# Pair pass of a four-layer graph network: row and square sums move from VectorE to TensorE, products keep six PSUM banks

## What is computed

```
hihj  = concatenate([x[src], x[dst]])                       # one row for each edge
exp_e = exp(silu(bn(hihj @ Wf + bf)))                       # one score for each edge
z     = silu(bn(einsum('ed,hdk->ehk', hihj, Wg) + bg))      # 128 values for each edge
h     = segment_sum(attention * z, dst);  out = bn(h) + x
bn(v) = (v - mean(v, axis=0)) * rsqrt(var(v, axis=0) + 1e-5) * gamma + beta
```

## Time and profile before

| | us |
|---|---|
| median of 3 runs | 12785.85 (12779.04 to 12810.68) |
| the profiled execution, its own time | 12782.4 |
| its span | 12780.6 |
| pair pass, from the first product (L1587) to the last reduction | 9613 to 11996 |

### The profile page before, as it was taken

The page is one execution under the profiler, slowest core; times in us unless marked ns, Lnnn a source line. Parts: engine busy times, 40 slices in busy tenths (PEclk is TensorE's granted clock), DMA queues, the critical chain, the costliest instruction groups (busy, mean ns, idle before and its releaser), DMA issues. The chain is left out here.

```text
span 12780.6 us, 88605 instructions
## 1 busy us (share of the span) xinstructions
PE 4468.3 (35%) x19462; PEld 2929.4 (23%) x19462; DVE 3466.1 (27%) x8115; ACT 3243.9 (25%) x7261; POOL 8419.5 (66%) x8885
## 2 busy tenths in 40 slices
PE   1222222432222223333333433333353333333587
PEld 0000000210000102111111322223352333333466
DVE  4000000200000111000000311212144565666799
ACT  3233333333333333233233300000020000101365
POOL 5666666566666665666666566666656666666698
PEclk5555555655555555555555555555575555555799
DMA  3222222222222223222222111111114444444444
GB/s 99 71 70 69 70 71 69 70 79 69 70 71 69 70 70 88 70 69 70 70 68 70 52 46 47 47 47 46 47 43 131 134 137 133 139 135 140 135 162 136
DMA packets 676226, 1070.09 MB, mean 84 GB/s; under 512 B 150832, under 2 KB 518725, under 8 KB 648853
## 3 DMA queue, kind: packets, MB, share of 16 engines
q0 software_dynamic: 329072, 676.05, 20.5%
q10 hardware_dynamic: 247712, 225.10, 5.4%
q1 hardware_dynamic: 98981, 163.50, 3.9%
HBM read 904.63 MB, written 161.05 MB: 83 GB/s over the span
## 5 line engine op out<-in xcount | busy, mean ns | idle before, releaser
L441 POOL DMA_INDIRECT big<-table_parts,tile_cols x4689 | 4452.7, 950 | 2339.9 <-issue 1390.5
L583 PE MATMUL psum<-big 128*128 x4992 | 1720.4, 470 | 4278.4 <-ACT big L541 2184.7
L441 POOL DMA_INDIRECT big<-ptable,tile_cols x1563 | 1521.4, 973 | 842.4 <-issue 464.5
L441 POOL DMA_INDIRECT big<-table,tile_cols x1563 | 1489.1, 953 | 729.4 <-issue 458.6
L583 PEld LDWEIGHTS psum<-big 128*128 128x128 bf16 x4992 | 596.5, 119 | 5125.3 <-issue 4914.7
L541 ACT ACTIVATE big<-big,ones 128x2048 bf16<-128x2048 bf16 x312 | 625.1, 2004 | 4401.6 <-remote 2958.0
L534 ACT ACTIVATE big<-iota_col,dl_tab 128x128 bf16<-128x128 f32 x4992 | 1513.0, 389 | 134.0 <-issue 99.4
L1587 PE MATMUL psum<-acc,big 128*128 x3328 | 891.0, 436 | 1488.6 <-issue 897.0
L651 PE MATMUL psum<-big 128*128 x3328 | 770.8, 361 | 1450.4 <-issue 1348.7
L563 DVE TENSOR_REDUCE acc<-psum 128x128 f32<-128x384 f32 (+1 forms) x196 | 109.5, 559 | 4173.3 <-remote 2631.0
L1587 PEld LDWEIGHTS psum<-acc,big 128*128 128x128 f32 x3328 | 729.2, 309 | 1650.1 <-issue 1639.6
(11 more groups left out here) (298 smaller groups left out, 4174.4 us busy)
## 6 DMA issues: line engine op xcount, KB each, us to landing
big<-dl_rows ACTq DMA_DIRECT2D x104, 1024.0 KB
zrows<-big ACTq DMA_DIRECT2D x104, 1024.0 KB
big<-zrows SPq DMA_DIRECT2D x104, 1024.0 KB
big<-table_parts,tile_cols POOLq DMA_INDIRECT x4689
table_parts<-big SPq DMA_DIRECT2D x42, 672.0 KB, 3.5
big<-table,tile_cols POOLq DMA_INDIRECT x1563
big<-ptable,tile_cols POOLq DMA_INDIRECT x1563
ptable<-big SPq DMA_DIRECT2D x14, 455.0 KB, 4.2
```

The costliest lines, as they stand in the source:

```text
L441: pool.indirect_dma_start(out=slots[:, t % (groups * GT), 0:width], out_offset=None, in_=tab, in_offset=bass.IndirectOffsetOnAxis(ap=idx_t ...
L583: last = nc.tensor.matmul(held, m, rows_t, start=False, stop=False, skip_group_check=True)
```

## The change

PE takes the sums. Two of the 8 PSUM banks become accumulators (`z_sum`, `z_sq_sum`, one partition, 4 x 128 columns each), and the products of the items go round the other six. In half q, after item 6, PE adds up half q - 1 by four products of a column of ones with a quarter of the half (4 items x 128 = 512 columns); after items 7, 9, 11 and 13 it adds up one quarter of the squares each. ACT squares quarter by quarter into two small buffers of their own, so it no longer waits for the store, and `zbuf` is not overwritten. DVE no longer reduces, and `half_sum` and `total` are gone. `load_dst` is issued for half q + 3 after the stores of half q, with its two waits moved inside. The statistics block folds the two accumulators by two reductions on one partition.

```
--- before.py
+++ after.py
@@ -23,7 +23,7 @@
 CW = 7
 ACW = F + 2
 ZW = ACW + 1
-Z_BANKS = 8
+Z_BANKS = 6
 PSLOTS = 4
 PASSES = 5
 LN_EPS = 1e-5
@@ -1494,20 +1494,25 @@
 
 
 
-        s_dl, s_compared, s_masked, s_in, s_part, s_summed, s_squared = (sem(n) for n in (
-            "z_dst", "z_dst_compared", "z_masks", "z_in_window", "z_half_summed", "z_totals", "z_squared"))
+        s_dl, s_compared, s_masked, s_in, s_summed, s_squared, s_sq_summed = (sem(n) for n in (
+            "z_dst", "z_dst_compared", "z_masks", "z_in_window", "z_summed", "z_squared", "z_squares_summed"))
         s_zout = [sem(f"z_out{h}") for h in range(2)]
         s_scores = sem("z_scores")
         no = 4
         items0 = no * NI
         onehot_t = onehot.rearrange("p (h u) f -> p h (u f)", h=2)
         dl_wide = work_flat.rearrange("p (h e) -> p h e", h=2)
-        totals = wide[:, 0:2, 0:F]
-        part = wide[:, 2:4, 0:F]
+        QUART = HALF // 4
+        QUARTS = HALF // QUART
+        squares = [big[:, RB + OB + WB + k * QUART * F:RB + OB + WB + (k + 1) * QUART * F].rearrange("p (u f) -> p u f", f=F) for k in range(2)]
+        assert 2 * QUART * F <= 224 + 11 * (NW + 1)
+        z_sum, z_sq_sum = (bank[Z_BANKS + k][0:1, 0:QUART * F].rearrange("p (u f) -> p u f", f=F) for k in range(2))
         in_win = sc16[:, 0:2, :]
         low = sc16[:, 2, :]
         PER = HALF // READY_STEP
-        SUM_AFTER, SQUARES_AFTER = 2, HALF - 2
+        SUM_AFTER = Z_BANKS
+        SQUARES_AFTER = [Z_BANKS + 1 + 2 * j for j in range(QUARTS)]
+        assert SQUARES_AFTER[-1] < HALF
         PARTS = HALF * P // 512
         ITEMS_PER_PART = HALF // PARTS
         with nc.Block() as block:
@@ -1532,21 +1537,6 @@
                         dve.wait_ge(s_in, q + 1)
                         nc.vector.scalar_tensor_tensor(in_win[:, q % 2, :], d, float(P), low, ALU.is_lt, ALU.mult).then_inc(s_masked, 1)
 
-                def half_sum(q, k):
-                    rows_of = zbuf[:, q % 2, :, 0:F].rearrange("p u f -> p f u")
-                    if k == 0:
-                        dve.wait_ge(s_added, PSLOTS + (q + 1) * HALF)
-                    else:
-                        dve.wait_ge(s_squared, q + 1)
-                    if q > 0:
-                        dve.wait_ge(s_summed, 2 * q - 1 + k)
-                    nc.vector.tensor_reduce(part[:, k, :], rows_of, AX.X, ALU.add).then_inc(s_part, 1)
-
-                def total(q, k):
-                    dve.wait_ge(s_part, 2 * q + k + 1)
-                    nc.vector.tensor_tensor(totals[:, k, :], totals[:, k, :], part[:, k, :], ALU.add).then_inc(s_summed, 1)
-
-                nc.vector.memset(totals, 0.0)
                 for j in range(PARTS):
                     compare(0, j)
                 for q in range(HALVES):
@@ -1557,6 +1547,8 @@
                     if q >= 2:
                         dve.wait_ge(s_zout[h], 16 * (q // 2))
                         dve.wait_ge(s_scores, q - 1)
+                        dve.wait_ge(s_summed, q - 1)
+                        dve.wait_ge(s_squared, (q - 1) * QUARTS)
                     for u in range(HALF):
                         n = q * HALF + u
                         if u % READY_STEP == 0:
@@ -1566,16 +1558,21 @@
                                                        bank[n % Z_BANKS][:, 0:ACW], ALU.mult, ALU.add).then_inc(s_added, 1)
                         if u % ITEMS_PER_PART == 1 and q + 1 < HALVES:
                             compare(q + 1, u // ITEMS_PER_PART)
-                        if q > 0 and u in (SUM_AFTER, SQUARES_AFTER):
-                            half_sum(q - 1, u // SQUARES_AFTER)
-                        if q > 0 and u in (SUM_AFTER + 1, SQUARES_AFTER + 1):
-                            total(q - 1, u // SQUARES_AFTER)
-                for k in range(2):
-                    half_sum(HALVES - 1, k)
-                    total(HALVES - 1, k)
 
             @block.tensor
             def _(pe):
+                def add_half(q):
+                    pe.wait_ge(s_added, PSLOTS + (q + 1) * HALF)
+                    for j in range(QUARTS):
+                        last = nc.tensor.matmul(z_sum, ones[:, 0:1], zbuf[:, q % 2, j * QUART:(j + 1) * QUART, 0:F],
+                                                start=q == 0 and j == 0, stop=False, skip_group_check=True)
+                    last.then_inc(s_summed, 1)
+
+                def add_squares(q, j):
+                    pe.wait_ge(s_squared, q * QUARTS + j + 1)
+                    nc.tensor.matmul(z_sq_sum, ones[:, 0:1], squares[j % 2], start=q == 0 and j == 0, stop=False,
+                                     skip_group_check=True).then_inc(s_sq_summed, 1)
+
                 for q in range(HALVES):
                     at = pair_values(pe, WIN, q, (NW - 1) * ACW)
                     for u in range(HALF):
@@ -1586,30 +1583,40 @@
                             pe.wait_ge(s_added, PSLOTS + n - Z_BANKS + 1)
                         nc.tensor.matmul(bank[n % Z_BANKS][:, 0:ACW], onehot_t[:, q % 2, u * P:(u + 1) * P],
                                          dyn(acc_flat, at[u], ACW), start=True, stop=True).then_inc(s_prod, 1)
+                        if q > 0 and u == SUM_AFTER:
+                            add_half(q - 1)
+                        if q > 0 and u in SQUARES_AFTER:
+                            add_squares(q - 1, SQUARES_AFTER.index(u))
+                add_half(HALVES - 1)
+                for j in range(QUARTS):
+                    add_squares(HALVES - 1, j)
 
             @block.scalar
             def _(act):
                 def load_dst(q):
+                    if q >= 2:
+                        act.wait_ge(s_compared, PARTS * (q - 1))
+                        act.wait_ge(s_dl, 16 * q)
                     act.dma_start(dl_wide[:, q % 2, :], dl_rows[q * HALF:(q + 1) * HALF, :].rearrange("i e -> (i e)").partition_broadcast(P)
                                   ).then_inc(s_dl, 16)
 
                 load_dst(0)
                 act.wait_ge(s_dl, 16)
                 load_dst(1)
+                load_dst(2)
                 for q in range(HALVES):
                     h = q % 2
-                    if q + 2 < HALVES:
-                        act.wait_ge(s_compared, PARTS * (q + 1))
-                        act.wait_ge(s_dl, 16 * (q + 2))
-                        load_dst(q + 2)
                     act.wait_ge(s_added, PSLOTS + (q + 1) * HALF)
                     act.dma_start(zrows[q], zbuf[:, h, :, 0:F]).then_inc(s_zout[h], 16)
                     nc.scalar.copy(score_tab[:, q * HALF:(q + 1) * HALF], zbuf[:, h, :, F])
                     nc.scalar.copy(weight_tab[:, q * HALF:(q + 1) * HALF], zbuf[:, h, :, SCW]).then_inc(s_scores, 1)
-                    act.wait_ge(s_zout[h], 16 * (q // 2 + 1))
-                    act.wait_ge(s_summed, 2 * q + 1)
-                    z = zbuf[:, h, :, 0:F]
-                    nc.scalar.activation(z, z, ACT.Square).then_inc(s_squared, 1)
+                    if q + 3 < HALVES:
+                        load_dst(q + 3)
+                    for j in range(QUARTS):
+                        n = q * QUARTS + j
+                        if n >= 2:
+                            act.wait_ge(s_sq_summed, n - 1)
+                        nc.scalar.activation(squares[j % 2], zbuf[:, h, j * QUART:(j + 1) * QUART, 0:F], ACT.Square).then_inc(s_squared, 1)
                 for h in range(2):
                     act.wait_ge(s_zout[h], 16 * (HALVES // 2))
                 act.wait_ge(s_dl, 16 * HALVES)
@@ -1619,19 +1626,22 @@
 
         s_v, s_root, s_wide, s_silu, s_exp, s_sums = (sem(n) for n in ("bn_steps", "bn_root", "bn_wide", "bn_silu", "bn_exp", "bn_sums"))
         mean, var, scale_r, shift_r = (rows[:, k, :] for k in (RT0, RT1, RT2, RT3))
-        z_stats = bank[5]
+        score_sums = bank[5][0:1, 0:2]
         scores_sq = work_flat[:, 0:NI]
         s_col, sq_col = (work_flat[:, NI + k:NI + k + 1] for k in range(2))
         with nc.Block() as block:
             @block.vector
             def _(dve):
-                step = Steps(dve, s_v, 0, 17)
+                step = Steps(dve, s_v, 0, 19)
                 step(nc.vector.tensor_reduce(s_col, score_tab, AX.X, ALU.add))
                 step(nc.vector.tensor_tensor(scores_sq, score_tab, score_tab, ALU.mult))
                 step(nc.vector.tensor_reduce(sq_col, scores_sq, AX.X, ALU.add))
                 dve.wait_ge(s_sums, 1)
-                step(nc.vector.tensor_scalar(mean, z_stats[0:1, 0:SCW], 1.0 / E, None, ALU.mult))
-                step(nc.vector.tensor_scalar(var, z_stats[0:1, SCW:2 * SCW], 1.0 / E, None, ALU.mult))
+                for row, sums, k in ((mean, z_sum, 0), (var, z_sq_sum, 1)):
+                    nc.vector.tensor_reduce(row[:, 0:F], sums.rearrange("p u f -> p f u"), AX.X, ALU.add)
+                    step(nc.vector.tensor_copy(row[:, F:SCW], score_sums[:, k:k + 1]))
+                for row in (mean, var):
```

(13 more changed lines are left out.)

## The result

The changed kernel takes 12845.0 us (12827.8 to 12853.6), the kernel before 12785.85 us: a ratio of 1.0044, 95% interval 1.0033 to 1.0055. It is slower by 59 us; 12696 us were forecast. The profiled execution took 12844.6 us (span 12842.8). Both kernels were run where queues creep, that is, where rows start far apart with nothing that holds them ("remote"), as the prediction describes. In some later sets of runs they don't, and the kernel before takes 11361 to 11377 us with nothing changed.

The account below looks back on a forecast made before the run. POOL was taken to set the pair pass's pace: 1985 us of gathers plus 359.5 us of waiting for slots. That wait's -91 and the statistics block's +1 gave -90, hence 12696 us (forecast's own range 12590 to 12760).

Parts of the forecast that it names:

- The sum: Pair pass: POOL's wait falls from 359.5 to 268.4 us, -91; with +1 for the statistics block, -90.
- Step 2: PE in the pair pass gains eight fp32 products a half; some 13 us a half, between 10.8 and 21.5.
- Step 3: Six banks for item products: DVE waits 1 to 4.5 us behind `add_half`; gain 0 to 7 us a half.
- Step 1: DVE in the pair pass loses reductions and adds, 832 us; 7.2 us a half remain, off a release's path.
- the ring: Pair pass slots, 32 against 64 in the weights pass: may keep more of POOL's wait, down to a gain of 30.
- rival B: PE becomes the bound at items 7 to 13 of each half: slower, 12870 us (12820 to 13100); chance 0.22.
- 1700 to 2200 named as a sign: PE's busy time in the pair pass, in us, expected after the change.
- Step 4: ACT squares in quarters, 4 x about 0.59 us for one of 1.92, without waiting for the store: costs nothing.
- Step 5: Last sums, after the last half's last add: 7 to 14 us, taken as 11, for 11.4 now; no change.
- Step 6: Statistics block: two reductions and two copies come in, two 128-column products go; +1 us (0 to 3).
- The gathers: Pair pass gathers are 0.02 us dearer than in the weights pass, 31 us in all, expected to stay.
- A: POOL's wait in the pair pass stays as it is: 12770 us, between 12750 and 12800; chance 0.20.

Follow-up runs that it names:

- fixed stretches: Constant reductions of fixed length put into DVE's queue, no creeping: kernel before 11952.4, changed 11693.4, one at a time 11561.9, without products 11372.3 us.
- holds: Stretches put into DVE's queue, of fixed length or until POOL stops: kernel before 11952.4 us (fixed, no creeping), 12939.8 us (until POOL stops, with creeping).
- the first edits: Changed kernel without products 11340.5, short products 11347.3, one at a time 11344.8; kernel before with six banks 11360.7; against 11361.8 us.
- the eight banks: Sums on TensorE with eight item banks kept, a 256-column product of ones ahead of each item product: 12862.8 us against 12791.9 of the kernel before.

## Why the prediction was wrong

The step that failed is its sum, "POOL's wait goes from 359.5 us to the 268.4 us of the pass whose consumer is light: -91". It went to 440.1. The sum has a term for DVE's lighter load and none for six banks and for the products of ones in PE's queue; steps 2 and 3 leave both to the sum, and the sum puts them at nothing. The runs with creeping give all three, as POOL's wait: six banks 359.5 to 433.6, +74; DVE's reductions gone 433.6 to 345.4, -88; the products of ones 345.4 to 440.1, +95; together +81. So the -91 was nearly right in size for what it stood for, and what failed is that the other two terms, +169 us, were left out.

- Step 1, DVE's load: 681 us busy in the pass, near the 600 named. "So DVE's work leaves the path of a release" is not what the runs show with creeping, where taking the reductions off won 133 us; without creeping DVE had not been on that path before either, since POOL never stopped.
- The level that the sum took from the weights pass, 268.4 us, was not reached even without any product: 345.4 us, with DVE at 673 us of work and six banks. That -88 is close to -91 is partly luck, since it is a fall from another level. The weights pass differs in 8 groups of slots for 4 and in a lighter DVE (428 us); I named the ring as a bound of the gain and did not follow it. Which of these holds the wait at 345 us was not tried.
- Step 2, PE's load: 9.3 us a half for the products (966/104) and 6.6 for the items, 15.9 in all, against the 13 of the estimate and its bounds of 10.8 and 21.5. The granted clock is 0.78 in the pass, and 0.86 without creeping: over the 0.75 under which rival B decides. PE's 1553 us in the pass lie under the 1700 to 2200 named as a sign.
 The Trainium skill's rule (TensorE: Matmul & The Clock Gate, section "HAM oscillation — how this bites in real kernels") holds in part here: one block of sums ran at 0.57, some 8 us after PE had stood 2.28 us for squares, and the one before it at 1.00.
- Step 3, six banks: PE's 3.5 to 7.0 us in `add_half` and DVE's wait of 1 to 4.5 us behind it were right in size (3.60 and 6.24; 2.96 and 5.15). "A gain of 0 to 7 us for a half" holds on the average of the pass: 8.0 us of reductions went, and DVE's waits for PE grew from 1.1 to 6.4 us a half (112.5 and 666.5 over 104), which leaves 2.7 us. But the fewer banks were priced only by that wait. In the kernel before they cost 77 us, though its waits for PE did not grow (86 us for 112).
- Step 4: ACT "costs nothing", but 303.6 us of PE's waits are for its squares; what they cost on the path was not tried. Step 5: from the last add to the last product 7 us, within 7 to 14, for 11.4. Step 6: from the first statistics reduction to the next stage's first operations 21.5 us before and 22.1 after, +0.6 for +1.
- The gathers: "31 us in all, I leave". Stops apart, the pass became 20 us shorter (2344.4 - 347.9 = 1996.5; 2389.0 - 413.0 = 1976.0), as the price of a gather fell from 973 to 959 ns. This was a gain left out.

In time, the same chain reads: two banks fewer +77; reductions away, with ACT's squares in quarters and `load_dst` moved along, -133; products one at a time +72; and +44 for the block of four and for the waits on the half's end and on ACT that the version one at a time also avoids. The last step compares two sets of runs. Each has some 20 us of uncertainty, and whether two banks cost the same where there are no reductions was not tried.

Of the rivals, B comes nearest in time and place: 12845 lies in its 12820 to 13100, and DVE's adds do wait for several hundred us (666.5) behind PE's queue. Its reason fails: the clock stood at 0.78, PE was busy for 1553 of 2391 us, and some of the loss is the banks'. A's sign, a wait over 340 us, is there as well, but its range, 12750 to 12800, is missed: it left out that the stops, though shorter (4.3 us for 5.7), become more.

Open: what makes queues creep, and what decides when they begin. Stops went from 61 to 96 with the change, and to 66 without the products; that the products bring more stops is shown (66 without, 90 one at a time, 96 as changed), in one trace each, and how they do is not. Also open is how two banks fewer bring 8 stops and 93 us of remote and issue.

## What to carry to other kernels

Work shed from an engine that follows a ring of gathers is worth only what it shortens inside the producer's stops (here 746 us shed, 104 won); outside them it turns into idle time, so the sum is made over the stops and not over the half. Such a sum needs a term for each thing that changes: here the two that were left out, the banks and the queue of the engine that takes the work, were together larger than the gain. Moving sums to TensorE puts them in front of the products that the shedding engine needs next; one at a time they cost less than in a block (190 us against 321 with fixed stretches, 72 against 116 with creeping). Banks taken from the lead cost 77 us, but the one version that kept all eight, with a product ahead of every item, was no faster (1.0052 against 1.0044 of its kernel before), and with creeping no version without holds that keeps the sums was faster than the kernel before. And a second trace of the kernel before, from another set of runs, tells what of the pace belongs to the kernel: here 1424 of 12786 us did not.

## What the runs showed of the hardware

Creeping is a condition of the set of runs and not of the kernel: the same program takes 12786 us with it and 11362 or 11377 without, and POOL's stops in all five passes (42, 47, 62, 56 and 61 in the trace before) go to none. Where it is, an add of 0.35 us can come each 5.5 us, and the matmul records of the weights pass start mostly 2.1 or 2.8 us apart (205 and 192 of the 523 distances between 1.5 and 12 us), where without it neither of the two distances comes at all. Of the seven sets of runs four had it and three had not, and the same chip had both (the first edits without, the eight banks with), so it does not go with the chip alone. The transfers that bring instructions are the same in the two conditions: 203 packets of 16 KB in one queue and 258 in the other, with it and without, and one of 16 KB takes about 1 us in both (median 0.98 and 1.05). In a set without creeping, a DVE that is late by its own work does not creep (the kernel before with holds: 184 us of "issue" and no "remote" over 2543 us), so lateness alone does not bring it on.

A product of ones, fp32, of 512 columns took 0.9 us at a granted clock of 1.00 (3.60/4), and 1.56 in the block at 0.57 (6.24/4). On average over its pass one of 512 columns took 1.16 us (clock 0.78) and one of 256 columns 0.68 us (1125.4/1664, clock 0.81), so halving the columns saved two fifths.

A DVE reduction of 2048 fp32 elements took 3.71 us where it reads elements 131 apart into 128 results, and 2.28 us where it reads adjacent ones into 16 results; the runs do not separate the two differences.
